# Values of two key heads projected in one pass in a causal attention with 16 query heads and 4 key heads

## The reference

```
B, L, D = 2, 1024, 256;  H, KV, HD = 16, 4, 128      # rep = H // KV = 4

def attention(x, wq, wk, wv, wo):                     # x: [B, L, D]
    q = (x @ wq).reshape(b, s, H, HD)
    k = (x @ wk).reshape(b, s, KV, HD)
    v = (x @ wv).reshape(b, s, KV, HD)
    q = apply_rope(q, cos, sin)
    k = apply_rope(k, cos, sin)
    k, v = jnp.repeat(k, rep, axis=2), jnp.repeat(v, rep, axis=2)
    scores = jnp.einsum('bqhd,bkhd->bhqk', q, k) / np.sqrt(HD)
    scores = jnp.where(causal[None, None], scores, jnp.finfo(scores.dtype).min)
    probs = jax.nn.softmax(scores, axis=-1)
    out = jnp.einsum('bhqk,bkhd->bqhd', probs, v).reshape(b, s, H * HD)
    return out @ wo

x = x + ga * attn1(h)        # attn1 ends with  mean @ fc_w.T + fc_b
h = layernorm(x) * (1 + cb) + sb
h2 = h + attention(rmsnorm(h, norm1_w), wq, wk, wv, wo);  then a mixture of experts
```

## Time and profile before

| what | value |
|---|---|
| median of three runs | 2584.09 us (2581.69 to 2587.95) |
| profiled execution, its own time | 2584.05 us |
| its span in the profile | 2582.2 us |
| PE, DVE, ACT, POOL busy | 91%, 55%, 43%, 44% of the span |
| attn2 | from about 1368 to 2269 us in the span |

### The profile page before, as it was taken

How to read it: one execution, slowest core, us unless ns; L and a number is a source line. 1 busy time by engine, 2 the same in 40 slices (tenths; PEclk the granted TensorE clock), 3 DMA queues, 4 the chain that set the end, 5 groups by cost and what they waited for, 6 DMA issues and landing times. The chain is left out here.

```text
span 2582.2 us, 34414 instructions
## 1 busy us (share of the span) xinstructions
PE 2355.5 (91%) x12718; PEld 1789.1 (69%) x12718; DVE 1420.6 (55%) x2476; ACT 1121.2 (43%) x1909; POOL 1139.1 (44%) x661
## 2 busy tenths in 40 slices
PE   6959999986999977999998989999999999949997
PEld 2329999973777756898896667777777777625554
DVE  6568888865222224545665865456456555463332
ACT  3467777722121113434443554646455454521221
POOL 0438999911332322343454445444544535223443
PEclk8979999997999997999999999999999999979999
DMA  6273181228312212000001000000000001055223
GB/s 242 98 294 84 58 326 58 95 72 274 96 30 34 33 36 79 1 1 1 1 1 54 21 1 21 21 1 21 1 21 5 18 9 33 1 160 154 46 42 64
DMA packets 109335, 168.33 MB, mean 65 GB/s; under 512 B 30547, under 2 KB 78675, under 8 KB 107093
## 3 DMA queue, kind: packets, MB, share of 16 engines
q1 hardware_dynamic: 94196, 145.35, 16.1%
q0 software_dynamic: 14976, 20.78, 4.9%
HBM read 115.94 MB, written 52.32 MB: 65 GB/s over the span
## 5 line engine op out<-in xcount | busy, mean ns | idle before, releaser
L638 POOL TENSOR_TENSOR mb_dbx<-mb_ud,mb_bb 128x1024 f32<-128x1024 f32 x128 | 302.0, 2363 | 58.7 <-DVE mb_h L496 42.4
L496 DVE TENSOR_TENSOR_SCAN mb_h<-ps,mb_dbx 128x1024 f32<-128x1024 f32 x128 | 292.2, 2288 | 49.8 <-ACT ps L608 38.8
L2115 POOL TENSOR_TENSOR a_e<-a_e,a_rc 128x1024 f32<-128x1024 f32 (+5 forms) x144 | 189.0, 1321 | 267.3 <-DVE a_rc L2031 266.9
L2282 PE MATMUL ps<-a_eT,a_v 128*128 128x512 f32 x576 | 296.4, 596 | 5.1 <-ACT a_eT L2159 5.1
L2041 DVE TENSOR_REDUCE a_mx<-ps 128x1 f32<-128x1024 f32 (+7 forms) x256 | 192.6, 752 | 176.9 <-PE ps L2261 176.0
L946 POOL DMA_INDIRECT e_acc<-e_hid,e_ids x78 | 123.7, 1585 | 370.9 <-DVE e_hid L1240 356.6
L2159 ACT ACTIVATE a_eT<-ps 128x512 f32<-128x512 f32 x288 | 171.2, 594 | 241.2 <-PE ps L2272 240.6
L740 PE MATMUL ps<-mb_dg,mb_hts 128*128 128x128 f32 x2048 | 251.5, 276 | 0.4
L740 PEld LDWEIGHTS ps<-mb_dg,mb_hts 128*128 128x128 f32 x2048 | 240.4, 193 | 1.9 <-issue 1.9
L1226 DVE COPY e_work<-ps 128x256 f32<-128x256 f32 x78 | 33.1, 425 | 356.4 <-PE ps L1064 356.4
L1792 POOL TENSOR_TENSOR a_elo<-a_e,a_ehi 128x1024 fp32r<-128x1024 f32 x48 | 117.8, 2453 | 227.0 <-ACT a_ehi L1649 113.8
(11 more groups left out here) (377 smaller groups left out, 5398.4 us busy)
## 6 DMA issues: line engine op xcount, KB each, us to landing
mb_bb<-mb_db_rows SPq DMA_DIRECT2D x16, 1024.0 KB, 12.4
mb_ddiag<-mb_dg SPq DMA_DIRECT2D x1, 8192.0 KB, 22.3
mb_dg<-mb_ddiag SPq DMA_DIRECT2D x8, 1024.0 KB, 12.9
e_wg<-in_g SPq DMA_DIRECT2D x8, 688.0 KB, 10.7
e_wu<-in_u SPq DMA_DIRECT2D x8, 688.0 KB, 11.4
e_wd<-in_d SPq DMA_DIRECT2D x8, 640.0 KB, 10.8
mb_dxa<-mb_bb SPq DMA_DIRECT2D x8, 512.0 KB, 2.6
mb_dz<-mb_xz SPq DMA_DIRECT2D x8, 512.0 KB, 2.9
```

The lines of the kernel that those rows point to most:

```text
L496: dve.tensor_tensor_scan(h[:, at % 2, :], pair(at % 2), dbx[:, at % 2, :], 0.0, ALU.mult, ALU.add).then_inc(s_h, 1)
L638: pool.tensor_tensor(dbx[:, at % 2, :], ud[:, kk % 2, 0, :], bb[:, n, :], ALU.mult).then_inc(s_dbx, 1)
L2115: pool.tensor_tensor(probs(i, h), probs(i, h), rc[:, q:q + 1].to_broadcast([P, (i + 1) * P]), ALU.mult).then_inc(s["en"], 1)
L2282: mm = pe.matmul(ps[:, 6 + rows[u, i] % 2, :], v[:, j, :], eT[:, k % ER, :], start=(j == 0), stop=(j == i))
```

## The change

The value columns of two neighbouring key heads are loaded together (256 columns; `WC` grows from 768 to 896), and at each even unit `values` runs twice with i = 0, 1, each 24 matmuls with 256 moving columns for half of the tokens. Odd units have no `values`; their `value` products read the other half of `v`. The weights are now split in four pieces before an even unit (256, 256, 128, 256 columns, the fourth at row 5) and in three before an odd one (256, 256, 128). `gafb` now holds one batch, lies in an unused part of `raw`, and is computed twice: `fold(0)` is DVE's chore at row (0,0,3) as before, `fold(1)` is its chore at (0,0,7), and the chores behind it (`centred`, `modulated`, `shift1`) come three rows later; POOL's first addition moves up from row (0,0,5) to (0,0,4); `product`, a buffer of unit 7, lies where cos was. The core of the diff:

```diff
-WC = (REP + 2) * HD
-WPIECE, WPIECES = 256, WC // 256
+WC = (REP + 3) * HD
+PIECES = ((0, 2 * HD), (2 * HD, REP * HD), (REP * HD, (REP + 1) * HD), ((REP + 1) * HD, WC))
+def pieces(u):
+    return len(PIECES) - u % 2
...
+    parts = [(wq, 0, REP * HD, kv), (wk, REP * HD, (REP + 1) * HD, kv), (wv, (REP + 1) * HD, WC, kv // 2)]
...
-            def fold():
-                dve.wait_ge(pre.s_mod[1], 16)
-                dve.wait_ge(s_fc, 32)
-                dve.tensor_tensor(gafb[:, :, :], mod[:, :, GA * D:(GA + 1) * D], over(fbw, B), ALU.mult).then_inc(s_gafb, 1)
+            def fold(b):
+                if b == 0:
+                    dve.wait_ge(s_fc, 32)
+                else:
+                    dve.wait_ge(s_fold, 1)
+                    dve.wait_ge(pre.s_mod[1], 16)
+                dve.tensor_tensor(gafb, mod[:, b, GA * D:(GA + 1) * D], fbw, ALU.mult).then_inc(s_gafb, 1)
...
-                    if (b, h, i) in ((0, 0, 5), (0, 2, 3)):
+                    if (b, h, i) in ((0, 0, 4), (0, 2, 3)):
...
-            weights = {(7, 3): 0, (6, 2): 1, (6, 5): 2}
+            weights = {(7, 3): 0, (6, 2): 1, (6, 5): 2, (5, 2): 3}
...
-                put("values", u, 0, 0)
+                if u % 2 == 0:
+                    put("values", u, 0, 0)
+                    put("values", u, 1, 0)
...
-                act.wait_ge(s["unit"], done["values", u - 1, 0, 0])
+                act.wait_ge(s["unit"], done["project", u - 1, REP, 0] if c < 3 else done["values", u - 2, 1, 0])
...
-                    for c in range(TB):
+                    for c in range(4):
                         for k in range(KC):
                             for x_, y_ in THREE:
-                                mm = pe.matmul(ps[:, o + c // 4, (c % 4) * P:(c % 4 + 1) * P],
-                                               hT[x_][:, k, c * P:(c + 1) * P], wh[y_][:, k, NPROJ * HD:WC],
+                                mm = pe.matmul(ps[:, o + c // 2, (c % 2) * 2 * HD:(c % 2 + 1) * 2 * HD],
+                                               hT[x_][:, k, (4 * i + c) * P:(4 * i + c + 1) * P], wh[y_][:, k, NPROJ * HD:WC],
```

More of the change, by code:

```diff
@@ L1353, in __init__ @@
         self.cos, self.sin, self.nwb, self.mask_f = part["cos"], part["sin"], part["nwb"], part["mask_f"]
+        self.spare = g.raw[:, at:at + D]
         self.s_x, self.s_mod = [sem(f"x{q}") for q in range(4)], [sem(f"mod{b}") for b in range(B)]
 def head_columns(pre, wq, wk, wv, kv):
-    return [(pre.w_s[:, :, c0:c1], w.rearrange("(k p) n -> p k n", p=P)[:, :, kv * (c1 - c0):(kv + 1) * (c1 - c0)])
-            for w, c0, c1 in ((wq, 0, REP * HD), (wk, REP * HD, (REP + 1) * HD), (wv, (REP + 1) * HD, WC))]
+    parts = [(wq, 0, REP * HD, kv), (wk, REP * HD, (REP + 1) * HD, kv), (wv, (REP + 1) * HD, WC, kv // 2)]
+    return [(pre.w_s[:, :, c0:c1], w.rearrange("(k p) n -> p k n", p=P)[:, :, n * (c1 - c0):(n + 1) * (c1 - c0)])
+            for w, c0, c1, n in parts[:pieces(kv) - 1]]
 def resume(nc, g, pre, acc):
@@ L1397, in attn1 @@
         raw = g.raw[:, :].rearrange("p (w k h e) -> p w k h e", w=3, k=KC, h=AH)
-        gafb = sb("gafb", [P, B, D])
+        gafb = pre.spare
         wm = [flat(w[:, :, :]).rearrange("p (a k d) -> p a k d", a=2 * AH, k=KC) for w in pre.wm]
@@ L1710, in small @@
                 dve.tensor_copy(pre.ident_b[:, :], ident[:, :]).then_inc(s_bf, 1)
-            chores = {0: [lambda: stats1(0), lambda: stats1(1), lambda: norm.spread(1, False), lambda: fold(), lambda: norm.inverse(1, 2),
+            chores = {0: [lambda: stats1(0), lambda: stats1(1), lambda: norm.spread(1, False), lambda: fold(0), lambda: norm.inverse(1, 2),
+                          lambda: None, lambda: None, lambda: fold(1),
                           *[lambda q=q: norm.centred(hs, x, TB + 2 * q, 2) for q in range(4)],
@@ L1895, in schedule @@
                         if u + 1 < U:
-                            if (i, j) in weights:
+                            if (i, j) in weights and weights[i, j] < pieces(u + 1):
                                 put("weights", u + 1, weights[i, j], 0)
@@ L1940, in normed @@
             return [scored[u, i, h] for h in range(REP)]
+        split_until = {u: sum(pieces(n) for n in range(1, u + 1)) for u in range(U)}
+        loaded_until = {u: sum(pieces(n) - 1 for n in range(1, u + 1)) for u in range(U)}
+        valued = {t[1:3]: n + 1 for n, t in enumerate(t for t in unit if t[0] == "values")}
         by_pool = {n: c + 1 for c, n in enumerate(n for (u, i, h), n in scored.items() if h < REP - 1)}
@@ L2175, in _ @@
                     act.wait_ge(s["unit"], done[what, u, i, h])
-                    act.activation(flat(v[:, :, :]), pair(unit[what, u, i, h]), ACT.Copy).then_inc(s["v"], 1)
+                    act.activation(v[:, 4 * i:4 * i + 4, :, :].rearrange("p c a d -> p (c a d)"), pair(unit[what, u, i, h]), ACT.Copy).then_inc(s["v"], 1)
                 elif what == "value" and h == i:
@@ L2278, in _ @@
                         if i == TB - 1:
-                            pe.wait_ge(s["v"], u + 1)
+                            pe.wait_ge(s["v"], valued[u - u % 2, 1])
                         if rows[u, i] > 1:
                             pe.wait_ge(s["ao"], rows[u, i] - 1)
-                    mm = pe.matmul(ps[:, 6 + rows[u, i] % 2, :], v[:, j, :], eT[:, k % ER, :], start=(j == 0), stop=(j == i))
+                    mm = pe.matmul(ps[:, 6 + rows[u, i] % 2, :], v[:, j, u % 2, :], eT[:, k % ER, :], start=(j == 0), stop=(j == i))
                     if j == i:
```

36 lines of the change are left out of this document (18 added, 18 removed).

## The result

The changed kernel takes 2561.36 us (median of four runs, 2556.69 to 2563.04), the kernel before 2582.89 us (four runs). The ratio is 0.9902, with a 95% interval of 0.9886 to 0.9919; the medians alone differ by 21.5 us, 0.83%, near the small end of that interval. The forecast was 2562.7 us. The profiled execution took 2562.03 us; its span is 2560.2 us, 22.0 less than before.

A forecast was written before the change was run, and what follows sets the result against it. From unit 1 of attn2 on, PE's own work was taken to set the time; in unit 0 DVE and POOL set part of the pace. 2584.05 - 21.4 + 1.5 + 0.2 - 1.6 = 2562.75, forecast 2562.7 us, range 2557 to 2571.

The forecast's parts named there:

- Odd units: attn2 units 1, 3, 5 and 7: without values, each start shrinks by 5.36 us, 21.4 us in all.
- Even units: attn2 units 0, 2, 4 and 6: 48 matmuls widened to 256 columns cost 0.4 us a unit, 1.5 us together.
- The start of an odd unit: First turn of row 7 in odd units waits 0.04 us for DVE's division, booked as 0.2 us for four units.
- The addition of gafb: attn1: with POOL's addition one row earlier, PE's wait for vlo near 1062 us vanishes, 1.6 us gained.
- Weights: POOL's weight pieces, with a fourth at row 5 before even units, are ready in time; booked at nothing.
- columns cost what they stream: Rival, chance 0.03: in even units a 256-column matmul costs two of 128, 5.36 us a unit; time 2582.5 us.
- the chain of row 7 becomes the wait: Rival, chance 0.13: odd units wait for DVE's division in row 7, four times 2 us; time about 2571.
- Unit 0 kept its rhythm: Rival, chance 0.12: unit 0 falls into another rhythm, one 4.84 us wait more or less; 2558 or 2567.5.
- The late fourth piece: Rival, chance 0.02: projections of units 2, 4 and 6 wait for the fourth weight piece; time above 2589.3 us.

The follow-up runs named there:

- e4: The kernel before with the narrow value projection in even units only, so odd units use the even key head's values; 2560.55 us.
- e3: The changed kernel with the wide value projection, both halves, in every unit, odd ones too; 2583.34 us.
- e5: The changed kernel with one unneeded row maximum on DVE before the division of row 7's last head in odd units; 2567.47 us.
- e6: The kernel before with one unneeded row maximum on DVE before the division of row 7's last head in odd units; 2587.98 us.
- e1: The kernel before with only POOL's first addition of gafb moved from row (0,0,5) to (0,0,4); 2581.54 us.
- e2: The changed kernel with POOL's first addition of gafb put back behind row (0,0,5); 2562.6 us.
- e8: The changed kernel with the fourth weight piece at row 4, just before the projection that needs it, in place of row 5; 2571.28 us.
- e7: The changed kernel with three unneeded row maxima on DVE before the division of row 7's last head in odd units; 2582.61 us.
- b1: The changed kernel with the last two residuals of attn1's second batch each in a row of its own and the statistics in one chore; 2555.21 us.
- b3: The changed kernel with both moves, those of b1 and b2; 2551.02 us.
- b2: The changed kernel with batch 1's norm spreading and ACT's root moved from unit 0 to beside unit 2's value projections; 2553.46 us.

## Why the prediction was right

The time came within 1.4 us of the forecast, and the mechanism is the one that was forecast. The terms one by one:

- **Odd units, -21.4 predicted.** -5.36, -5.44 and -5.44 measured at units 1, 3 and 7, and e4, which does nothing else, shows 5.34 on average over three. The reading of the earlier trace rows held: an odd unit loses the 48 starts and pays 0.63 us where it paid 0.28.
- **Even units, +1.5.** 0.3 at unit 0, 0.45 and 0.47 at two others; 0.34 a unit in e3, 0.29 from e4. Predicted 0.4 each from the earlier trace rows. The term is right, a little high by two of the measures. In the changed kernel the starts are 0.12 us apart, as said:

```profile
1617.49 0.28 PE L2259 MATMUL ps<-h_whhi,h_hTlo 128*128 128x256 f32 x1
1617.61 0.28 PE L2259 MATMUL ps<-h_whhi,h_hThi 128*128 128x256 f32 x1
1617.73 0.28 PE L2259 MATMUL ps<-h_whlo,h_hThi 128*128 128x256 f32 x1
```

- **The start of an odd unit, +0.2.** No wait is booked, the turn comes 1.70 us after the score (1.75 forecast). The wait of 0.04 us that was read from the rows was right to within 0.1: e5 shows that the next 1.25 us are paid in full, e6 that the kernel before had cover for them.
- **The addition of gafb, -1.6.** -1.75 in the change; e1 and e2 move the same 1.75 us, there and back, by the one line.
- **Weights, 0.** No wait of PE for POOL's split; e8 shows what it would look like.

The sum is right partly by luck. The start of attn1 came 1.4 us late in this execution, and the clock near 1210 us gave back 1.5; neither was in the working, and they cancel. The first is scatter. The second need not be: it came in every trace that has both the changed attn1 and the moved addition, and in no other. If it belongs to the change, the term for attn1 was too small by half, 1.6 us in place of 3.25.

**The rivals.** That columns cost what they stream is out: e3 would have been 20 us slower. That the chain of row 7 becomes the wait didn't happen, but it was the right one to fear, and e5 gives its true price: its nearest row, 2 us late for four units, would have cost 8 us without the clock, and what the clock added in e7 was not in it. Unit 0 kept its rhythm: its waits of 2.32 and 4.84 us are 2.32 and 4.82 in the changed kernel. The late fourth piece needed a place one row later than the change gives it.

## What to carry to other kernels

Cost a change in matmul shape by the distance of starts in a stretch of the same type and shape in the kernel's own trace, and not by its columns: here, from 128 to 256 columns, a matmul with its own weight load went from 0.112 to 0.120 us, so that joining two saved nearly a whole one. When a block of work is taken out of the engine that bounds the kernel, write down what else ran in its shadow and by how much that was early; here it fitted to 0.1 us, and an extra microsecond would have been paid four times. And where DVE and POOL meet, move one of them by a row before shortening either: one line in an order moved 1.75 us here, and a few small instructions in another place 6.6 us of B and C in the one trace of it.

## What the runs showed of the hardware

**A wait costs more than its length when the clock falls behind it, and with the same code it falls in one execution and not in another.** Behind waits of 3.60 us in e7 the granted clock fell at all four odd starts. Behind three waits of 2.6 to 2.7 us in e8 it did so once. b1 and b3 have the same code up to their wait of 2.64 and 2.63 us for `kTlo`, shown above, and behind it the starts are 0.43 us apart in b1 and 0.23 in b3. The changed kernel and b2 have the same code up to a wait of 2.02 us for `kTlo`, and again the clock fell in the first only.

The wait near 1208 us is another matter. It is 2.8 us long in all eleven traces that have it. Behind it PE runs at the lower clock in the kernel before, e1, e2, e4 and e6, and at the full one in the changed kernel, e3, e5, e7, e8 and b2. The first five lack the changed attn1 (the later norm chores and the second `fold`), the moved addition or both; the last six have both. Before, then after:

```profile
1207.94 0.80 PE L1559 MATMUL ps<-a_hThi,h_wmhi 128*128 128x512 f32 x1 [2.77 <-DVE h_qklo L1746]
1208.53 0.63 PE L1559 MATMUL ps<-a_hTlo,h_wmhi 128*128 128x512 f32 x1
1208.96 0.63 PE L1559 MATMUL ps<-a_hThi,h_wmlo 128*128 128x512 f32 x1
```

```profile
1207.68 0.50 PE L1566 MATMUL ps<-a_hThi,h_wmhi 128*128 128x512 f32 x1 [2.76 <-DVE h_qklo L1757]
1208.01 0.40 PE L1566 MATMUL ps<-a_hTlo,h_wmhi 128*128 128x512 f32 x1
1208.25 0.40 PE L1566 MATMUL ps<-a_hThi,h_wmlo 128*128 128x512 f32 x1
```

That alone was worth 1.5 us, nearly as much as the addition of `gafb`. A split of five against six without an exception doesn't look like chance. The wait comes at 211.3 us after the start of attn1 in the changed kernel and at 213.0 before, but at 211.2 in e1, where the clock fell, so the place alone doesn't decide it either. What does was not tried, and each kernel has only one profiled execution.

**DVE instructions of 0.17 us that take up to 2.3.** Eight elements a partition cost 2.26 us at 1485.48, 0.17 at 1603.60. At the first place POOL runs `wmlo` from 1485.37 for 2.34 us, and both end within 0.04 us of each other (1487.74 and 1487.71); at the second POOL runs nothing. All five long ones of unit 0 lie beside an instruction of POOL and end 0.02 or 0.03 us after one of its instructions, and those between 1487.78 and 1489.16, where POOL is idle, take 0.17 us. The size of such an instruction didn't tell how long it held up the engine.
